# Query parts stored once and repeated by the loads, in an attention and mixture-of-experts layer

## The chip, the cores and the metric
The kernel runs on one core of one Trainium2 chip. The metric is the device time of one execution in microseconds, and the median of several executions is quoted. A core has five engines that run their own streams of instructions and meet at semaphores: TensorE (PE), VectorE (DVE), ScalarE (ACT), GpSimd (POOL) and SyncE (SP). SP does no arithmetic here; it issues nearly all DMAs. 16 DMA engines move the data.

## The reference
One layer on x of 32 batches x 512 tokens x 256. Attention with 16 heads of 16 in 4 key groups (4 query heads share a key head), rotary positions and a causal mask, then a mixture of 16 experts of which each token uses 2:

```python
q = (x @ Wq + bq).reshape(b, t, 16, 16).transpose(0, 2, 1, 3)
k = (x @ Wk + bk).reshape(b, t, 4, 16).transpose(0, 2, 1, 3)   # v likewise
k = jnp.repeat(k, 4, axis=1)
q, k = _rope(q), _rope(k)
scores = jnp.einsum('bhtd,bhsd->bhts', q, k) / scale
scores = jnp.where(causal, scores, -jnp.inf)
attn = jnp.einsum('bhts,bhsd->bhtd', softmax(scores), v)
...
x = x + layernorm(attention(layernorm(x)))
x = x + layernorm(ffn(layernorm(x)))
```

## The kernel before
Each query and key is cut into PARTS = 3 bf16 numbers whose sum is the float32 value. TensorE forms a score as a sum of six products of parts. For that the parts are stacked along the partitions, in six blocks of DH = 16: a tile of 96 partitions (KR) of queries, `qs`, against one of keys, `ks`. BLOCKS says which part of the query and of the key stands in each block:

```python
BLOCKS = [(0, 1), (0, 0), (0, 2), (1, 0), (1, 1), (2, 0)]
Q_BLOCKS = [slice(0, 3), slice(3, 5), slice(5, 6)]
K_BLOCKS = [slice(1, 6, 2), slice(0, 5, 4), slice(2, 3)]
```

So query part 0 stands in blocks 0 to 2, part 1 in 3 and 4, part 2 in 5. The parts are made elsewhere on the partitions: POOL's `split` writes `q_parts` (two halves of 128 partitions, each half eight of the 16 dimensions times 16 heads) and `k_parts`. They reach their blocks through DRAM: SP's `store_parts` writes them to `q_stack_dram` and `k_stack_dram`, with a copy for each block, and `load_stacks` reads them back with the block and the dimension on the partitions, first `ks` (L531) and then one load for each of four groups g of four heads (L535). Three more partitions, 96 to 98, hold the negated row maxima in parts; `load_negmax` (L540) loads them for two groups at a time, from `k_parts_negmax_t`, of which they are 24 partitions.

The work is software-pipelined over batches. The list TURN is one turn, four groups g times 11 slots e; each engine walks the same list for c in TURNS, and a step has an offset that says for which batch it is done. In turn c the scores for exp (L804, `score_exp`) are those of batch c, the scores whose maxima are taken (L788, `score_max`) those of batch c + 1 for groups 0 to 2 (c for group 3), and the projection and splits (L834 and `split`) those of batch c + 2. `load_stacks(c + 1)` stands at slot (0, 5), the first `score_max` of batch c + 1 at (1, 1), `load_negmax` of the second pair of groups at (1, 5) and its first use at (2, 0); the stores of the query halves stand at (2, 4) and (3, 7), that of the keys at (3, 10), and `load_x_res` just before `load_stacks`. Each engine works its stream strictly in this order. Waits: SP waits in `load_stacks` for all parts of the batch (`parts_stored`) and for the last exp of the batch that used the buffer; TensorE waits in `score_max` for the group's load (`q_stack_loaded`), in `score_exp` for `negmax_loaded`. After the last turn of attention come the rest of the expert tiles, with no loads of stacks.

Of the kernel before, what the change touches and what calls it, by code (L numbers as in the profile page):

```python
# [20 lines left out]
BF16 = mybir.dt.bfloat16  # L21
# [7 lines left out]
B, T, D = 32, 512, 256  # L29
NT = T // P  # L30
NC = D // P
H, G, DH = 16, 4, 16
HG = H // G
E, I = 16, 128
TOKENS = B * T
PARTS = 3
# [4 lines that stand above are left out]
KR = len(BLOCKS) * DH  # L41
# [168 lines left out]
D_TAIL = first_of_tail(FOR_DVE, D_NO)  # L210
A_TAIL = first_of_tail(FOR_ACT, A_NO)
SPLITS = 5
PER_STORE = 16 * 3 * PARTS

LAST_TURN = ALL_TILES + 2 + 12
FINALS_FROM, FINALS_OVER = TILES[0] + 8, LAST_TURN - TILES[0] - 9
# [88 lines left out]
def layer(nc, a, out):  # L305
    ctx = ExitStack()
    with ctx:
        def sb(name, shape, dt=F32):
            return ctx.enter_context(nc.sbuf_tensor(name, shape, dt))

        def sem(name):
            return ctx.enter_context(nc.semaphore(name))

        def dram(name, shape, dt=F32):
            return nc.dram_tensor(name, shape, dt, kind="Internal").ap()


        q_stack_dram = dram("q_stack_dram", [2, len(BLOCKS), DH, H, T], BF16)
        k_stack_dram = dram("k_stack_dram", [2, len(BLOCKS), DH, G, T], BF16)
        h2_dram = dram("h2_dram", [B, T, D])  # L320
        sorted_dram = [dram(f"sorted_dram{k}", [LIST, ROW]) for k in range(2)]
        y_dram = dram("y_dram", [2 * TOKENS + ALL_TILES * P, D])


        wq = sb("wq", [P, NC, 2, P])
        wkv = sb("wkv", [P, NC, P])
        bq = sb("bq", [P, 2])
        bk = sb("bk", [P, 1])
        rope = sb("rope", [P, 4, T])
        wo = sb("wo", [P, NC, D])  # L330
        bo = sb("bo", [P, D])
        gate_w = sb("gate_w", [P, NC, 2 * E])
        act_bias = sb("act_bias", [P, 3])
        wgu = sb("wgu", [P, E + 1, NC, 2 * I])
        wd = sb("wd", [P, E + 1, D])
        ident = sb("ident", [P, P])
        ident_bf = sb("ident_bf", [P, P], BF16)
        mask_max = sb("mask_max", [P, P], BF16)
        mask_exp = sb("mask_exp", [P, P], BF16)
        before = sb("before", [P, P], BF16)  # L340
        ones_bf = sb("ones_bf", [P, P], BF16)
        iota_e = sb("iota_e", [P, E])
        token = sb("token", [P, NT])

        h2_std, h2_mean = sb("h2_std", [P, B, NT]), sb("h2_mean", [P, B, NT])
        tile_no, row_no = sb("tile_no", [P, TQ, E]), sb("row_no", [P, 1])
        first_rows = rope[:, :, :].rearrange("p k t -> p (k t)")[:, 0:ROW]
        counts = sb("counts", [P, NT + 1, E])

        pool_cell, dve_cell = sb("pool_cell", [1, 2]), sb("dve_cell", [1, 2])  # L350
        zero_col = sb("zero_col", [P, 1])

        weights_in = sem("weights_in")
        consts = sem("consts")
        experts_in = sem("experts_in")
        h2_stored = sem("h2_stored")
        doubled = sem("doubled")
        scattered = [sem(f"scattered{k}") for k in range(2)]
        lists_begun = sem("lists_begun")

        tile_plan = sb("tile_plan", [P, 2, 3, TQ])
        keep = ctx
        programs(nc, a, out, locals())


def programs(nc, a, out, v):
# [13 lines left out]
    with ctx:  # L380
        def sb(name, shape, dt=F32):
            return ctx.enter_context(nc.sbuf_tensor(name, shape, dt))
# [4 lines left out]
        def sem(name):  # L387
            return v["keep"].enter_context(nc.semaphore(name))
# [6 lines left out]
        q_parts = sb("q_parts", [P, 2, PARTS, T], BF16)  # L395
# [3 lines left out]
        k_parts = k_parts_negmax_t[0:G * DH]  # L399
        negmax_t = k_parts_negmax_t[G * DH:G * DH + PARTS * 2 * HG, 0:2]  # L400
        qs = sb("qs", [P, 2, H, T], BF16)
# [9 lines left out]
        heads = sb("heads", [P, T // 32, 2 * DH])  # L411
# [51 lines left out]
        parts_stored = [sem(f"parts_stored{k}") for k in range(2)]  # L463
        k_stack_loaded = [sem(f"k_stack_loaded{k}") for k in range(2)]
        q_stack_loaded = [[sem(f"q_stack_loaded{k}{g}") for g in range(G)] for k in range(2)]
# [19 lines left out]
    def _(sp):  # L485
# [22 lines left out]
        def store_parts(b, unit):  # L508
            sp.wait_ge(split_steps, SPLITS * (3 * b + unit + 1))
            if unit == 0 and b >= 2:  # L510
                sp.wait_ge(k_stack_loaded[b % 2], 16 * (b // 2))
                for g in range(G):
                    sp.wait_ge(q_stack_loaded[b % 2][g], 16 * (b // 2))
            for part in range(PARTS):
                if unit < 2:
                    half = slice(unit * DH // 2, (unit + 1) * DH // 2)
                    dst = q_stack_dram[b % 2, Q_BLOCKS[part], half].rearrange("k d h t -> (d h) k t")
                    src = q_parts[:, unit, part, :]
                else:
                    dst = k_stack_dram[b % 2, K_BLOCKS[part]].rearrange("k d g t -> (d g) k t")  # L520
                    src = k_parts[:, part, :]
                n = [Q_BLOCKS, K_BLOCKS][unit == 2][part]
                copies = len(range(n.start, n.stop, n.step or 1))
                sp.dma_start(dst, src.unsqueeze(1).to_broadcast([src.shape[0], copies, T])) \
                    .then_inc(parts_stored[b % 2], 16)

        def load_stacks(b):
            sp.wait_ge(parts_stored[b % 2], PER_STORE * (b // 2 + 1))
            if b >= 2:
                sp.wait_ge(a_taken, A_NO["E", (G - 1, NE - 1), b - 2] + 1)  # L530
            sp.dma_start(ks[0:KR, b % 2], k_stack_dram[b % 2].rearrange("k d g t -> (k d) g t")) \  # L531
                .then_inc(k_stack_loaded[b % 2], 16)
            for g in range(G):
                heads = slice(g * HG, (g + 1) * HG)
                sp.dma_start(qs[0:KR, b % 2, heads], q_stack_dram[b % 2, :, :, heads].rearrange("k d h t -> (k d) h t")) \  # L535
                    .then_inc(q_stack_loaded[b % 2][g], 16)

        def load_negmax(b, pair):
            sp.wait_ge(a_taken, A_NO["mt", pair, b] + 1)
# [53 lines left out]
    def _(pool):  # L593
# [36 lines left out]
        def split(b, unit, stage):  # L630
# [11 lines left out]
            if stage == 1 and unit == 0 and b >= 1:  # L642
                pool.wait_ge(parts_stored[(b - 1) % 2], PER_STORE * ((b - 1) // 2 + 1))
            if stage:
# [127 lines left out]
    def _(pe):  # L772
# [3 lines left out]
        def score_max(b, g, u):  # L776
            j, h0, nh, width, stride = MAX_UNITS[u]
            number = D_NO["M", (g, u), b]
            if u == 0:
                if g == 0:  # L780
                    pe.wait_ge(k_stack_loaded[b % 2], 16 * (b // 2 + 1))
                pe.wait_ge(q_stack_loaded[b % 2][g], 16 * (b // 2 + 1))
            if number >= 2:
                pe.wait_ge(d_taken, number - 1)
            for k in range(nh):
                h = g * HG + h0 + k
                at = k * stride
                pe.matmul(ps_d[:, number % 2, at:at + width], qs[0:KR, b % 2, h, j * P:(j + 1) * P],  # L788
                          ks[0:KR, b % 2, g, 0:width], start=True, stop=False)
                ins = pe.matmul(ps_d[:, number % 2, at + j * P:at + (j + 1) * P], ident_bf[:, :], mask_max[:, :],  # L790
                                start=False, stop=True)
            ins.then_inc(d_full, 1)
# [100 lines left out]
        for c in TURNS:  # L893
            for at, step, arg, ahead in TURN:
                b = c + ahead
                if step == "side" and (c, at) in TILE_IN:
                    tile_turn(TILE_IN[c, at])
                if not has(step, b):
                    continue
                if step == "E":  # L900
                    score_exp(b, *arg)
                elif step == "M":
                    score_max(b, *arg)
                elif step == "P":
                    weigh(b, *arg)
                elif step in FOR_DVE:
                    for_dve(step, arg, b)
                elif step in FOR_ACT:
                    for_act(step, arg, b)
# [419 lines left out]
def expert_phases(nc, a, out, v):  # L1329
# [89 lines left out]
    def front_is_free(eng):  # L1419
# [5 lines left out]
        for k in range(2):  # L1425
            eng.wait_ge(v["parts_stored"][k], PER_STORE * B // 2)

# [530 lines left out]
```

## Time and profile before

| what | value |
|---|---|
| median of 3 runs | 2555.26 us (2533.58 to 2560.37) |
| the profiled execution, its own time | 2581.22 us |
| its span, first to last instruction | 2579.4 us |
| mean granted TensorE clock | 0.968 |
| TensorE, DVE, POOL, ACT busy | 91%, 77%, 65%, 55% of the span |
| DMA moved | 387.60 MB, mean 150 GB/s |

The profiled execution has 2 us around its span, and took 26 us more than the median of the runs. Busy shares are averages over two stages, attention (to about 1750 us) and experts; what a change in attention is worth must be read from turns of that stage. In the rows below a name such as `x<-in_x` gives what is written and what is read; L plus a number is a line of the kernel; SPq means an issue by SP.

### The profile page before, as it was taken

The numbers are of one execution on the slowest core, as the hardware profiler recorded it, in microseconds if no ns is written. First come the engines' busy times: TensorE is split into PE (matmuls) and PEld (weight loads), VectorE is DVE, ScalarE is ACT, GpSimd is POOL, SyncE is SP. The second block draws the span as 40 slices with busy tenths as digits, with TensorE's granted clock in tenths as the row PEclk, the third lists the DMA queues.
The fourth block names the chain that finished last, engine by engine and source line by source line (L and its number), as shares of the span: only waits on it lengthen the run. The fifth ranks groups of instructions, "written<-read, shape, count | busy, mean of one in ns | idle before, by whom it ended". The sixth has DMA issues, their size and how long they took to land.

```text
span 2579.4 us, 58722 instructions
## 1 busy us (share of the span) xinstructions
PE 2335.8 (91%) x18042; PEld 1502.2 (58%) x18042; DVE 1985.7 (77%) x5145; ACT 1417.2 (55%) x3248; POOL 1682.2 (65%) x2888
## 2 busy tenths in 40 slices
PE   4969999999999999998999999998779999999987
PEld 2545555555555555555555555554557787777754
DVE  5758888888888888888888888885455555788778
ACT  1546566665666656665566655665334444555544
POOL 2536667767677667766677756653656665677766
PEclk7889999999999999999999999998989999999999
DMA  4355544455444554455434445332344465677757
GB/s 127 89 146 150 158 143 134 129 153 167 129 130 147 156 153 128 121 147 152 122 116 125 141 136 154 109 106 88 113 140 140 147 201 186 194 232 223 230 196 248
DMA packets 289392, 387.60 MB, mean 150 GB/s; under 512 B 25856, under 2 KB 239872, under 8 KB 288960
## 3 DMA queue, kind: packets, MB, share of 16 engines
q1 hardware_dynamic: 263072, 312.51, 41.9%
q0 software_dynamic: 26016, 71.34, 7.5%
q8 instruction: 154, 2.52, 0.4%
q14 instruction: 150, 1.23, 0.2%
HBM read 193.14 MB, written 172.26 MB: 142 GB/s over the span
## 4 chain that ended last, share of the span: by engine, by line
PE 39%; POOL 31%; DMA 11%; issue 9%; DVE 5%; SPq 2%; ACT 1%; another core or an unknown queue 1%; POOLq 0%; ACTq 0%; DVEq 0%
PE bank L1611 9%; DMA qs<-q_stack_dram 7%; PE bank L1625 5%; POOL q_parts L646 4%; PE ps_d L834 4%; POOL rest L648 4%; DMA k_stack_dram<-k_parts_negmax_t 3%; PE ps_d L841 3%; PE ps_d L788 3%; PE bank L1593 2%; POOL sorted_dram L715 2%; POOL guess L686 2%; POOL k_parts_negmax_t L646 2%; POOL q_parts L648 2%; POOL heads L726 2%
## 5 line engine op out<-in xcount | busy, mean ns | idle before, releaser
L931 ACT ACTIVATE probs<-ps_a 128x512 f32<-128x512 f32 (+1 forms) x1408 | 716.2, 560 | 497.4 <-PE ps_a L806 446.0
L1053 DVE TENSOR_REDUCE negmax<-ps_d 128x2 f32<-128x768 f32 (+3 forms) x768 | 779.4, 1033 | 173.3 <-PE ps_d L790 159.2
L788 PE MATMUL ps_d<-ks,qs 96*128 96x128 bf16 (+3 forms) x2048 | 492.6, 307 | 125.0 <-DMA qs<-q_stack_dram 57.7
L804 PE MATMUL ps_a<-qs,ks 99*128 99x512 bf16 (+3 forms) x2048 | 525.2, 304 | 8.6 <-ACT probs L931 2.2
L790 PE MATMUL ps_d<-mask_max,ident_bf 128*128 128x128 bf16 x2048 | 400.6, 224 | 0.0
L806 PE MATMUL ps_a<-mask_exp,ident_bf 128*128 128x128 bf16 x2048 | 391.5, 221 | 0.0
L788 PEld LDWEIGHTS ps_d<-ks,qs 96*128 96x128 bf16 x2048 | 204.7, 100 | 294.1 <-issue 134.3
L1523 POOL DMA_INDIRECT y_dram<-ysb,to_row x286 | 285.6, 999 | 105.3 <-POOL pool_cell L251 52.4
L818 PE MATMUL ps_out<-probs,va 128*32 128x512 f32 (+3 forms) x4096 | 332.9, 443 | 2.5 <-DVE by_token L1096 2.3
L804 PEld LDWEIGHTS ps_a<-qs,ks 99*128 99x128 bf16 x2048 | 199.9, 98 | 207.0 <-issue 65.3
L1611 PE MATMUL bank<-wgu,rows_t 128*128 x1144 | 300.3, 386 | 0.0
L715 POOL DMA_INDIRECT sorted_dram<-h,slot x256 | 256.5, 1002 | 66.0 <-issue 65.1
L1826 DVE TENSOR_TENSOR hid<-bank,gate 128x128 f32<-128x128 f32 x286 | 82.2, 287 | 192.2 <-ACT gate L1731 174.9
L806 PEld LDWEIGHTS ps_a<-mask_exp,ident_bf 128*128 128x128 bf16 x2048 | 202.2, 99 | 28.2 <-issue 20.7
L1625 PE MATMUL bank<-wd,hid_t 128*128 x572 | 181.2, 399 | 40.4 <-issue 21.4
L1611 PEld LDWEIGHTS bank<-wgu,rows_t 128*128 128x128 f32 x1144 | 198.4, 194 | 16.1
L790 PEld LDWEIGHTS ps_d<-mask_max,ident_bf 128*128 128x128 bf16 x2048 | 204.9, 100 | 0.4 <-issue 0.3
L818 PEld LDWEIGHTS ps_out<-probs,va 128*32 128x32 f32 x4096 | 108.1, 110 | 144.9 <-issue 78.5
L251 POOL TENSOR_TENSOR pool_cell<-zero_col 1x1 f32<-1x1 f32 x318 | 62.4, 196 | 196.9 <-DVE slot L1192 105.6
L726 POOL TENSOR_TENSOR heads<-by_token,inverse 128x256 f32<-128x256 f32 x128 | 80.7, 630 | 147.7 <-DVE inverse L1098 141.6
L1731 ACT ACTIVATE gate<-bank 128x128 f32<-128x128 f32 x286 | 79.7, 279 | 139.0 <-PE bank L1611 96.6
L1625 PEld LDWEIGHTS bank<-wd,hid_t 128*128 128x128 f32 x572 | 102.4, 192 | 84.9 <-issue 74.0
(206 smaller groups left out, 4409.3 us busy)
## 6 DMA issues: line engine op xcount, KB each, us to landing
qs<-q_stack_dram SPq DMA_DIRECT2D x128, 384.0 KB
rows<-sorted_dram SPq DMA_DIRECT2D x286, 129.0 KB
y_in<-y_dram SPq DMA_DIRECT2D x32, 1024.0 KB
q_stack_dram<-q_parts SPq DMA_DIRECT2D x64, 384.0 KB, 2.6
x_in<-in_x SPq DMA_DIRECT2D x32, 512.0 KB
q_stack_dram<-q_parts SPq DMA_DIRECT2D x64, 256.0 KB, 2.9
x<-in_x SPq DMA_DIRECT2D x32, 512.0 KB, 4.4
h_dram<-h SPq DMA_DIRECT2D x32, 512.0 KB
```

What stands on the lines that cost most here:

```text
L646: steps.did(pool.tensor_tensor(parts[k], r, zero_col[0:n, :].to_broadcast([n, T]), ALU.add))
L715: pool.indirect_dma_start(out=sorted_dram[b // SPLIT_AT][:, :], in_=h2[:, k, j, :], in_offset=None, out_offset=bass.IndirectOffsetOnAxis(a ...
L788: pe.matmul(ps_d[:, number % 2, at:at + width], qs[0:KR, b % 2, h, j * P:(j + 1) * P], ks[0:KR, b % 2, g, 0:width], start=True, stop=False)
L790: ins = pe.matmul(ps_d[:, number % 2, at + j * P:at + (j + 1) * P], ident_bf[:, :], mask_max[:, :], start=False, stop=True)
L804: pe.matmul(ps_a[:, number % 3, at:at + width], ks[0:KM, b % 2, g, j * P:(j + 1) * P], qs[0:KM, b % 2, g * HG + h0 + k, j * P:T], start=Tr ...
L806: ins = pe.matmul(ps_a[:, number % 3, at:at + P], ident_bf[:, :], mask_exp[:, :], start=False, stop=True)
L818: ins = pe.matmul(ps_out[32 * h:32 * h + 32, j * P:T], va[:, b % 3, j, g * 32:(g + 1) * 32], probs[:, at:at + width], start=(j == 0), stop ...
L931: act.activation(probs[:, at:at + nh * width], ps_a[:, number % 3, 0:nh * width], ACT.Exp) \
L1053: dve.tensor_reduce(negmax[:, g // 2, j, at:at + nh], src, AX_X, ALU.max, negate=True) \
L1523: pool.indirect_dma_start(out=y_dram[:, :], in_=ysb[:, k, :], in_offset=None, out_offset=bass.IndirectOffsetOnAxis(ap=to_row[k][:, 0:1].bi ...
L1611: ins = pe.matmul(ps_gu[t % 2][:, 0:2 * I], rows_t[:, t % 2, c, :], wgu[:, expert[t], c, :], start=(c == 0), stop=(c == NC - 1))
L1625: pe.matmul(ps_y[t % 2][:, 0:D], hid_t[:, t % 2, :], wd[:, expert[t], :], start=True, stop=True) \
```

## The change
A half of the query parts is stored by one transfer that writes the three parts once each, in place of three transfers that write six copies. `q_stack_dram` shrinks from six blocks to three parts. Each group's load becomes three loads, one for each part; the one of part 0 writes 48 partitions and reads its 16 rows three times, that of part 1 writes 32 and reads twice, that of part 2 writes 16. All three count on the semaphore of the group. The keys are stored and loaded as before.

```diff
-PER_STORE = 16 * 3 * PARTS
+PER_STORE = 16 * (2 + PARTS)
...
-        q_stack_dram = dram("q_stack_dram", [2, len(BLOCKS), DH, H, T], BF16)
+        q_stack_dram = dram("q_stack_dram", [2, PARTS, DH, H, T], BF16)
...
+            if unit < 2:
+                half = slice(unit * DH // 2, (unit + 1) * DH // 2)
+                sp.dma_start(q_stack_dram[b % 2, :, half].rearrange("k d h t -> (d h) k t"), q_parts[:, unit]) \
+                    .then_inc(parts_stored[b % 2], 16)
+                return
             for part in range(PARTS):
-                if unit < 2:
-                    half = slice(unit * DH // 2, (unit + 1) * DH // 2)
-                    dst = q_stack_dram[b % 2, Q_BLOCKS[part], half].rearrange("k d h t -> (d h) k t")
-                    src = q_parts[:, unit, part, :]
...
             for g in range(G):
                 heads = slice(g * HG, (g + 1) * HG)
-                sp.dma_start(qs[0:KR, b % 2, heads], q_stack_dram[b % 2, :, :, heads].rearrange("k d h t -> (k d) h t")) \
-                    .then_inc(q_stack_loaded[b % 2][g], 16)
+                for part, n in enumerate(Q_BLOCKS):
+                    sp.dma_start(qs[n.start * DH:n.stop * DH, b % 2, heads],
+                                 q_stack_dram[b % 2, part, :, heads].unsqueeze(0)
+                                 .to_broadcast([n.stop - n.start, DH, HG, T])) \
+                        .then_inc(q_stack_loaded[b % 2][g], 16)
...
-                pe.wait_ge(q_stack_loaded[b % 2][g], 16 * (b // 2 + 1))
+                pe.wait_ge(q_stack_loaded[b % 2][g], 16 * PARTS * (b // 2 + 1))
```

Only SP's stream changes; the other engines have the same instructions in the same order. The first place is SP's stores of one batch, from the load of x to the first store of keys. Before (the sizes are those of the side written, partitions first):

```order
L545 DMA x_in<-in_x 128x4x256
L524 DMA q_stack_dram<-q_parts 128x3x512
L524 DMA q_stack_dram<-q_parts 128x2x512
L524 DMA q_stack_dram<-q_parts 128x512
L540 DMA qs<-k_parts_negmax_t 3x8x512
L524 DMA q_stack_dram<-q_parts 128x3x512
L524 DMA q_stack_dram<-q_parts 128x2x512
L524 DMA q_stack_dram<-q_parts 128x512
L524 DMA k_stack_dram<-k_parts_negmax_t 64x3x512
```

And now:

```order
L547 DMA x_in<-in_x 128x4x256
L516 DMA q_stack_dram<-q_parts 128x3x512
L542 DMA qs<-k_parts_negmax_t 3x8x512
L516 DMA q_stack_dram<-q_parts 128x3x512
L523 DMA k_stack_dram<-k_parts_negmax_t 64x3x512
```

Each half's three stores are one; its 3 is now the number of parts and no longer that of copies of part 0. The load of the maxima keeps its place. The second place is SP's loads of the stacks of one batch, behind the key stores. Before:

```order
L524 DMA k_stack_dram<-k_parts_negmax_t 64x3x512
L524 DMA k_stack_dram<-k_parts_negmax_t 64x2x512
L524 DMA k_stack_dram<-k_parts_negmax_t 64x512
L531 DMA ks<-k_stack_dram 96x2048
L535 DMA qs<-q_stack_dram 96x2048 x4
L545 DMA x_in<-in_x 128x4x256
```

And now, up to the end of the first group:

```order
L523 DMA k_stack_dram<-k_parts_negmax_t 64x3x512
L523 DMA k_stack_dram<-k_parts_negmax_t 64x2x512
L523 DMA k_stack_dram<-k_parts_negmax_t 64x512
L530 DMA ks<-k_stack_dram 96x2048
L535 DMA qs<-q_stack_dram 48x1x2048
L535 DMA qs<-q_stack_dram 32x1x2048
L535 DMA qs<-q_stack_dram 16x2048
```

The last three rows come three times more, for groups 1 to 3, before the load of x (L547): four issues became twelve.

## Rows read from the trace of the kernel before

**Rows 1.** The page's head: span, then busy time, share and instructions.

```profile
span 2579.4 us, 58722 instructions
PE 2335.8 (91%) x18042; PEld 1502.2 (58%) x18042; DVE 1985.7 (77%) x5145; ACT 1417.2 (55%) x3248; POOL 1682.2 (65%) x2888
```

**Rows 2.** Busy time by stretch: one turn; six microseconds inside the query loads.

```profile
core 0: us, PE busy (x) PEld busy (x) DVE busy (x) ACT busy (x) POOL busy (x), PEclk, DMA share, GB/s
1000.00:1052.60 52.60, 49.70 (x463) 29.54 (x460) 45.69 (x107) 33.06 (x69) 37.34 (x63) 1.00 0.47 137
1003.00:1009.00 6.00, 3.85 (x29) 2.86 (x28) 3.57 (x9) 1.61 (x3) 3.75 (x8) 1.00 1.01 266
```

**Rows 3.** Waits of the whole span: total us, times, longest.

```profile
PE ps_d L788 <- DMA qs<-q_stack_dram: 57.7, 29, 4.0
```

**Rows 4.** The chain that ended last, 990 to 1060: start, us, what.

```profile
997.95 2.44 DMA k_stack_dram<-k_parts_negmax_t
1000.40 0.34 SPq L531
1000.79 6.77 DMA qs<-q_stack_dram
...
1013.98 3.60 PE ps_d L834 x8
...
1053.39 5.90 DMA qs<-q_stack_dram
```

**Rows 5.** TensorE in order of time: start, us, instruction, idle before and releaser.

```profile
1007.65 0.22 PE L788 MATMUL ps_d<-ks,qs 96*128 96x128 bf16 x1 [2.15 <-DMA qs<-q_stack_dram]
...
1021.71 0.39 PE L804 MATMUL ps_a<-qs,ks 99*128 99x512 bf16 x1
```

**Rows 6.** SP's issues in order of time, same turn.

```profile
1000.40 0.34 SPq L531 DMA_DIRECT2D ks<-k_stack_dram  x1
1000.79 2.68 SPq L535 DMA_DIRECT2D qs<-q_stack_dram  x4
1003.52 1.22 SPq L545 DMA_DIRECT2D x_in<-in_x  x1
1015.07 0.79 SPq L540 DMA_DIRECT2D qs<-k_parts_negmax_t  x1
...
1041.07 1.62 SPq L524 DMA_DIRECT2D q_stack_dram<-q_parts  x3
```

**Rows 7.** DVE, then POOL, in order of time, same turn.

```profile
1026.67 0.28 DVE L1034 BATCH_NORM_AGGREGATE moments<-stats 128x2 f32<-128x6 f32 x3
...
1028.05 0.20 POOL L684 TENSOR_TENSOR var<-moments,eps 128x4 f32<-128x4 f32 x1
```

**Rows 8.** DMA packets of the span; queues with packets, MB, share of 16 engines.

```profile
DMA packets 289392, 387.60 MB, mean 150 GB/s; under 512 B 25856, under 2 KB 239872, under 8 KB 288960
q1 hardware_dynamic: 263072, 312.51, 41.9%
q0 software_dynamic: 26016, 71.34, 7.5%
```

**Rows 9.** DMA issues: engine, count, KB each, median us from issue to landing.

```profile
qs<-q_stack_dram SPq DMA_DIRECT2D x128, 384.0 KB
...
q_stack_dram<-q_parts SPq DMA_DIRECT2D x64, 384.0 KB, 2.6
...
q_stack_dram<-q_parts SPq DMA_DIRECT2D x64, 256.0 KB, 2.9
...
q_stack_dram<-q_parts SPq DMA_DIRECT2D x64, 128.0 KB, 2.8
...
qs<-k_parts_negmax_t SPq DMA_DIRECT2D x64, 24.0 KB
```

**Rows 10.** TensorE's restart after the start-up; then windows with granted clock.

```profile
43.11 0.27 PE L788 MATMUL ps_d<-ks,qs 96*128 96x128 bf16 x1 [17.97 <-issue]
...
44.00:48.00 4.00, 3.54 (x19) 2.14 (x17) 2.99 (x4) 0.00 (x0) 0.00 (x0) 0.50 1.02 259
48.00:52.00 4.00, 4.00 (x7) 1.64 (x7) 1.70 (x2) 0.00 (x0) 0.00 (x0) 0.68 0.05 16
```

More of the change, by code:

```diff
@@ L512, in store_parts @@
                 for g in range(G):
-                    sp.wait_ge(q_stack_loaded[b % 2][g], 16 * (b // 2))
-            for part in range(PARTS):
-                if unit < 2:
-                    half = slice(unit * DH // 2, (unit + 1) * DH // 2)
-                    dst = q_stack_dram[b % 2, Q_BLOCKS[part], half].rearrange("k d h t -> (d h) k t")
-                    src = q_parts[:, unit, part, :]
[L519 to L522, printed above, removed]
+                    sp.wait_ge(q_stack_loaded[b % 2][g], 16 * PARTS * (b // 2))
+            if unit < 2:
[3 more added lines that the diff above has]
+                return
+            for part in range(PARTS):
+                n = K_BLOCKS[part]
+                dst = k_stack_dram[b % 2, n].rearrange("k d g t -> (d g) k t")
                 copies = len(range(n.start, n.stop, n.step or 1))
-                sp.dma_start(dst, src.unsqueeze(1).to_broadcast([src.shape[0], copies, T])) \
+                sp.dma_start(dst, k_parts[:, part, :].unsqueeze(1).to_broadcast([G * DH, copies, T])) \
                     .then_inc(parts_stored[b % 2], 16)
```

## The prediction

> **What bounds the kernel now.** I read the page's head first: TensorE is busy for 2335.8 of 2579.4 us [rows 1]. In the attention stage one batch is one turn of 52.6 us, and in a turn it is busy for 49.7 [rows 2]. That looks like a TensorE bound, so I went on to the waits. TensorE waits 29 times for the load of the query stack, 57.7 us in all, 2.0 us each [rows 3]. The chain of work in time shows how that wait is made, and that it closes a loop from turn to turn: the query projection (L834) feeds DVE and then some 30 us of POOL splits, the last store of key parts lands 2.44 us after its issue, SP issues the load of the key stack and then that of the first query group, and 6.77 us later (5.90 in the next turn) TensorE goes on [rows 4]. So two things of nearly equal length hold a turn: TensorE's own work, and this loop through POOL and two DMA round trips. Whatever lengthens the first group's load lengthens the loop by as much, from the first microsecond on. What shortens it helps by 2 us a turn at most, since then TensorE's work is the bound.
>
> **How a transfer is laid on the DMA engines.** This decides the case. The only transfer of the kernel before whose two sides differ in their outer size is that of the row maxima (L540): 3 partitions of 8 rows on one side, 24 partitions on the other. Each engine that takes part adds one small packet at the end of a transfer, and these can be counted. SP issues 1086 transfers and POOL 542 indirect ones (the sum of the counts of the DMA view; the loops give the same), 64 of them L540 [rows 9], and 640 data packets (rows of bk, bq, act_bias and gate_w) are under 512 B. The page has 25856 packets under 512 B [rows 8]. With 16 engines for all: 640 + 16 x 1628 = 26688, which is 832 = 64 x 13 too many. With 3 engines for each L540 it comes out to the packet. So a transfer is cut by the outer sizes as its patterns list them, and is not spread over the 24 rows that it has. The new loads list 48 partitions on the side of qs and an outer step of 3 (the repeat, then 16 rows) on the side of DRAM, and 32 with 2 for the second part. If both sides count, these run on 3 and on 2 engines. If the destination alone did (the row fits that too), they would run on 16. I take the first, because a share must be whole on both sides and L540's source with 24 was held to 3.
>
> The Trainium skill, "DMA: Bandwidth & Descriptors", section "Why a DMA increments its semaphore by 16 and not by 1", speaks against this change: the number of engines is the largest up to 16 that divides the outermost sizes of both patterns, and they are the lowest-numbered ones. By it the new loads have 3 and 2 engines, and by it L540 has 3, with which the packet count agrees; no row here shows the numbers of the engines.
>
> **What the change removes.** Per batch four of six q stores and 768 of 1536 KB written ([rows 9]: 384 + 256 + 128 KB a half become 384). I cost the saving at nothing: the q1 stores are issued at 1041.07 in 1.62 us [rows 6], while the key parts that the loads wait for are stored when POOL is done with them, so that the next query load is issued only at 1053.39 [rows 4]. What hides the stores is POOL's chain. Bound of a gain: emptier engines might let the key store land sooner than its 2.44 us; stores of 384, 256 and 128 KB land in 2.6, 2.9 and 2.8 [rows 9], so size does little, and I allow 0.2 us a turn, 6 us.
>
> **What it adds, in issues.** Eight more issues a batch on SP, at 2.68 us for four [rows 6] 0.67 us each or less. Two of them stand in the first group's load, 1.3 us, beside transfers that take longer: nothing. Behind them in SP's queue stand the load of x and L540, 11.5 us later [rows 6].
>
> **What it adds, in time of the engines.** Bytes and rows of 4 KB are as before: 96 rows a group. Before, each engine had 6 of them. Now the two lowest engines have 16 + 16 + 1 = 33. Price of a row: between 1003 and 1009 only such loads run, at 266 GB/s with a share of 1.01 [rows 2], so 16.5 GB/s an engine and 0.25 us for 4 KB, all 16 pulling at once. In the light traffic of the indirect queue, 71.34 MB took 7.5% of 16 x 2579.4 = 3095 us [rows 8]: 23.0 GB/s, 0.178 us. With three engines at work the new load is nearer to the second; I take 0.178 and keep 0.25 as the far end. By the same skill page's section "Specifications" (about 27 GiB/s an engine) a row would be 0.141 us and the whole sum about 140 us in place of the 323 below; no row here shows that rate.
>
> First term, **the load of group 0**. From the issue of the key load (call it S, 1000.40) to TensorE's restart (1007.65) are 7.25 us [rows 5, 6]. Of these the engine worked on 6 rows of ks and 6 of q, 12 x 0.25 = 3.0; 4.25 us are start, rest of an earlier load, and completion. After: 4.25 + (6 + 33) x 0.178 = 4.25 + 6.9 = 11.2. So +3.9 us, on the loop, with nothing to hide it (far end: 39 x 0.25 gives +6.75).
>
> Second term, **the row maxima behind the query loads**. L540 for the second pair is issued at S + 14.7 [rows 6] and uses the same engines. In the turn shown TensorE does not wait for it before [rows 5]. Now the lowest engine has first 6 + 4 x 33 = 138 rows, 24.6 us; the load of x, 32 rows of 1 KB, 1.4; six of POOL's eight scatters a turn, which stand at slots (0, 9) and (0, 10) (26016 / 542 = 48 packets each [rows 8], of which 32 data: 2 an engine), 12 x 0.178 = 2.1; its own 8 rows, 0.4. With 4.25 that is S + 32.8. TensorE needs it for the first exp scores of group 2, 14.06 us after its restart (1021.71 - 1007.65, [rows 5]), so at S + 25.3. It waits 7.5 us. Of that, does the loop feel it? DVE's moments, which stand behind the next maxima, are ready at 1026.95 and POOL takes them at 1028.05 [rows 7]: 1.1 us of slack, then POOL's chain is late by 6.4. What is queued behind the waiting matmul is all of TensorE's stream, with DVE's maxima and POOL's splits. (Far end at 0.25: ready at S + 44.3, needed at S + 28.1, 16.2 of wait, 15.1 on the loop. Near end: nothing reaches the loop.)
>
> Groups 1 to 3 land 33 x 0.178 = 5.9 us apart and are needed a quarter of a turn, 13 us, apart: no wait.
>
> Third term, **the clock**. After an idle stretch of 17.97 us TensorE restarts at 43.11 at granted 0.50, and 48 to 52 has 0.68 [rows 10], so full speed from about 50.6: 7.4 us at 1.2 GHz, 3.7 lost. After the 2.15 us wait it was at 1.00 [rows 2, 5]. Two waits of 6 and 7.5 us a turn lie between these rows. I take 0 and keep 2 x 3.7 a turn, 229 us, as the other bound.
>
> **Sum.** 3.9 + 6.4 = 10.3 us a turn; 31 turns with both terms and one with the first: 319 + 4 = 323 us. The expert stage is not touched. Against the profiled execution, 2581.2 + 323 = 2904; it stood 26 us over the median of 2555.3, and against the median I forecast **2878 us**.
>
> **Rivals.**
> - Only the first term counts: the maxima come late, but the turn has grown and POOL had more air than I give it. 32 x 3.9 = 125, so 2680. Against it: no slack over 1.1 us in [rows 7].
> - Everything dearer: the clock falls at each wait (2878 + 229 = 3107), or a row stays at 0.25 us (31 x 21.9 + 7 = 686, so 3241). For it: the low clock after the start. Against it: only three engines pull.
> - Other side, **the loads are spread over all 16 engines** because the destination's 48, 32 and 16 decide. It decides as soon as the engine count of the first part is 16. Then the transfers are as before, the stores are halved, and the time is between -6 us (landing of the key parts) and +43 (32 x 1.34 us, if the two more issues delay the first group in full): 2549 to 2598, likeliest near 2565. For it: the packet count fits this reading too. Against it: L540's 24 rows did not help it, and its rule would have to ignore one side.
> - That the change moves other bytes than it says is excluded by the shapes: 128x3x512 stored, 48, 32 and 16 rows of 2048 loaded.
>
> **How the numbers follow.** Forecast (three engines, both terms, clock or price partly in it, 2760 to 3110) 0.65; first term only or little more (2620 to 2760) 0.15; dearer than 3110, 0.09; spread over 16, 0.11. The range that leaves out the last two is 2660 to 3110. A difference under 1% (25 us) can't be told from none here, with runs from 2533.6 to 2560.4. Slower by over 1%: 0.65 + 0.15 + 0.09 and 0.03 of the last case, 0.92; within 1%: 0.06; faster: 0.02.
>
> **What would show it.** In the profile after: packets under 512 B. 128 stores fewer take 2048 away, and the loads have (3 + 2 + 16) x 128 = 2688 in place of 2048, so 24448; spread over 16 it would be 27904. TensorE's wait for qs<-q_stack_dram about 6 us, 32 times, and a new wait for qs<-k_parts_negmax_t, 31 times, about 7. The DMA share falls from about 1.0 to 0.2 for some 20 us after the loads' issue. A turn of 63 us. If turns are 56 to 57, the second term is wrong; if the share stays at 1.0 in the loads, the first step is; if granted clock in attention falls well below 0.97, the third term is in play.

## The result, and the profile after

The changed kernel takes 2827.39 us (2824.37 to 2836.7), against 2557.41 us for the kernel before with one more run counted (2533.58 to 2560.37). The ratio, taken over all runs, is 1.109 of the kernel before (95% interval 1.102 to 1.115); the quotient of the medians is 1.106. The forecast was 2878, slower. Its profiled execution has a span of 2822.6 us, against 2579.4 [rows 1]. The kernels of the experiments ran on chips on which the kernel before took 2580 to 2590 us, so each is compared by its ratio to the kernel before on the same chip.

The page after, its head and its DMA rows (they answer to [rows 1] and [rows 8]):

```profile
span 2822.6 us, 58850 instructions
PE 2405.7 (85%) x18042; PEld 1568.4 (56%) x18042; DVE 1993.2 (71%) x5145; ACT 1424.1 (50%) x3248; POOL 1680.7 (60%) x2888
...
DMA packets 263410, 362.44 MB, mean 128 GB/s; under 512 B 24449, under 2 KB 213889, under 8 KB 262977
...
q1 hardware_dynamic: 237088, 287.34, 33.9%
q0 software_dynamic: 26016, 71.34, 6.8%
```

The packets under 512 B are read first, since they tell how the new loads are laid out: 24449, where 3 and 2 engines ask for 24448 and 16 engines for 27904. 25 MB fewer were moved, and nothing came of it.

The waits of the whole span (us in total, times, longest), to be held against [rows 3]:

```profile
POOL var L686 <- DVE moments L1036: 373.5, 92, 30.7
...
PE ps_d L790 <- DMA qs<-q_stack_dram: 161.6, 29, 7.1
...
PE ps_a L806 <- DMA qs<-k_parts_negmax_t: 108.6, 31, 8.0
```

The query load is waited for 5.6 us each time in place of 2.0, 103.9 us more. The wait for the row maxima is new but for 0.2 us: 31 times, 3.5 us. Together these waits are 212.5 us; the span grew by 243.2. TensorE's busy time also grew, by 69.9 us, with the same number of instructions, and its other waits shrank. DVE and POOL have no more work than before; the time in which POOL waits for DVE's moments grew from 100.5 us to 373.5, which is how TensorE's lateness reaches the loop.

The chain of work in order of time, through one turn (start, us, what; [rows 4] is its match):

```profile
1035.05 2.43 DMA k_stack_dram<-k_parts_negmax_t
1037.50 0.34 SPq L530
1037.88 0.77 SPq L535
1038.70 0.68 SPq L535
1039.42 8.76 DMA qs<-q_stack_dram
1048.27 0.26 PE ps_d L790
...
1057.31 10.27 DMA qs<-k_parts_negmax_t
1067.63 0.39 PE ps_a L806
```

From the issue of the key load, 1037.50, to TensorE's restart are 10.77 us where they were 7.25. The chain now runs a second time through a DMA: the load of the row maxima, 24 KB, takes 10.27 us from its issue. The explanation, tested below, is that it stands behind the query loads in the queues of its three engines. TensorE's stream (idle before, and what ended it) and POOL's, in the same turn:

```profile
1048.27 0.26 PE L790 MATMUL ps_d<-ks,qs 96*128 96x128 bf16 x1 [5.67 <-DMA qs<-q_stack_dram]
...
1067.63 0.39 PE L806 MATMUL ps_a<-qs,ks 99*128 99x512 bf16 x1 [2.48 <-DMA qs<-k_parts_negmax_t]
...
1073.79 0.20 POOL L686 TENSOR_TENSOR var<-moments,eps 128x4 f32<-128x4 f32 x1 [2.34 <-DVE moments L1036]
```

Before, POOL took the moments 20.40 us after TensorE's restart [rows 5, 7]; now 25.52. With 3.5 us from the first wait, 5.1 from there to the moments and 0.6 behind them, the turn has 61.9 us in place of 52.6. The view by stretches shows the turn and the pieces after its two waits (the columns of [rows 2]):

```profile
1037.50:1099.40 61.90, 53.66 (x464) 32.83 (x461) 45.93 (x107) 33.31 (x70) 37.38 (x64) 0.92 0.37 111
1040.00:1048.00 8.00, 2.59 (x14) 1.65 (x11) 2.95 (x9) 1.19 (x2) 5.18 (x9) 0.97 0.51 155
1048.00:1052.00 4.00, 3.73 (x21) 3.04 (x22) 1.56 (x2) 0.60 (x1) 1.92 (x2) 0.50 0.51 169
1052.00:1057.00 5.00, 5.00 (x40) 3.37 (x39) 2.77 (x6) 1.76 (x4) 0.00 (x0) 0.77 0.51 157
1057.00:1062.00 5.00, 5.00 (x26) 2.67 (x24) 4.78 (x12) 1.58 (x4) 2.47 (x8) 1.00 0.28 95
...
1067.00:1072.00 5.00, 4.37 (x29) 3.12 (x30) 2.03 (x4) 2.03 (x4) 4.21 (x4) 0.66 0.09 26
```

Two things are to be seen. The DMA share while the loads run, 0.51, is half of what it was [rows 2], although as many bytes are asked for. And the granted clock is 0.50 (1.2 GHz) for the 4 us after the wait of 5.67 us, and low again (0.66 in the mean of 5 us) after the second wait, of 2.48 us: the same matmuls take longer just where the loop hangs on them.

### The profile page after: what moved, and what is told of

It reads as the page before. It is cut to its first block, busy times and chain, and to the rows that moved or that the text cites. A ratio compares the mean times of both kernels' runs of the same rounds, so it can differ in the third digit from the quotient of the medians.

```text
span 2822.6 us, 58850 instructions
## 1 busy us (share of the span) xinstructions
PE 2405.7 (85%) x18042; PEld 1568.4 (56%) x18042; DVE 1993.2 (71%) x5145; ACT 1424.1 (50%) x3248; POOL 1680.7 (60%) x2888
## 2 busy tenths in 40 slices
DMA packets 263410, 362.44 MB, mean 128 GB/s; under 512 B 24449, under 2 KB 213889, under 8 KB 262977
## 4 chain that ended last, share of the span: by engine, by line
PE 48%; DMA 24%; POOL 12%; issue 6%; DVE 5%; SPq 4%; ACT 1%; POOLq 0%; ACTq 0%; DVEq 0%
DMA qs<-k_parts_negmax_t 12%; DMA qs<-q_stack_dram 9%; PE bank L1613 8%; PE ps_d L790 6%; PE ps_a L806 6%; PE bank L1627 4%; PE ps_out L820 4%; PE ps_d L843 3%; PE ps_d L792 3%; DMA k_stack_dram<-k_parts_negmax_t 3%; PE ps_d L836 3%; POOL k_parts_negmax_t L648 2%; PE bank L1595 2%; PE ps_a L808 2%; SPq L523 2%
## 5 line engine op out<-in xcount | busy, mean ns | idle before, releaser
L790 PE MATMUL ps_d<-ks,qs 96*128 96x128 bf16 (+3 forms) x2048 | 541.1, 330 | 216.9 <-DMA qs<-q_stack_dram 161.6
L806 PE MATMUL ps_a<-qs,ks 99*128 99x512 bf16 (+3 forms) x2048 | 553.9, 319 | 116.7 <-DMA qs<-k_parts_negmax_t 108.6
L792 PE MATMUL ps_d<-mask_max,ident_bf 128*128 128x128 bf16 x2048 | 444.0, 241 | 0.0
L790 PEld LDWEIGHTS ps_d<-ks,qs 96*128 96x128 bf16 x2048 | 224.3, 110 | 389.9 <-issue 267.8
L808 PE MATMUL ps_a<-mask_exp,ident_bf 128*128 128x128 bf16 x2048 | 402.9, 226 | 0.0
L806 PEld LDWEIGHTS ps_a<-qs,ks 99*128 99x128 bf16 x2048 | 206.2, 101 | 322.5 <-DMA qs<-k_parts_negmax_t 130.8
L686 POOL TENSOR_TENSOR var<-moments,eps 128x4 f32<-128x4 f32 x96 | 19.3, 201 | 375.8 <-DVE moments L1036 373.5
L792 PEld LDWEIGHTS ps_d<-mask_max,ident_bf 128*128 128x128 bf16 x2048 | 224.5, 110 | 0.4 <-issue 0.3
L808 PEld LDWEIGHTS ps_a<-mask_exp,ident_bf 128*128 128x128 bf16 x2048 | 208.2, 102 | 28.2 <-issue 21.2
L1627 PE MATMUL bank<-wd,hid_t 128*128 x572 | 179.4, 396 | 28.7 <-issue 19.1
L843 PE MATMUL ps_d<-wo,headst 128*128 128x256 f32 x512 | 158.3, 463 | 0.8 <-DVE place L1179 0.8
```

What stands on the lines that cost most here:

```text
L806: pe.matmul(ps_a[:, number % 3, at:at + width], ks[0:KM, b % 2, g, j * P:(j + 1) * P], qs[0:KM, b % 2, g * HG + h0 + k, j * P:T], start=Tr ...
L808: ins = pe.matmul(ps_a[:, number % 3, at:at + P], ident_bf[:, :], mask_exp[:, :], start=False, stop=True)
L843: ins = pe.matmul(ps[:, k * D:(k + 1) * D], headst[:, c, j * P:(j + 1) * P], wo[:, c, :], start=(c == 0), stop=(c == NC - 1))
L1627: pe.matmul(ps_y[t % 2][:, 0:D], hid_t[:, t % 2, :], wd[:, expert[t], :], start=True, stop=True) \
```

## The experiments

To compare turns, I took from SP's issues in order of time all issues of the key load between 300 and 1700 us and the first matmul of the new batch behind each; the last such turn of each kernel is left out, and the means are in this table. "Restart" is the time from the key load's issue to that matmul, "maxima" that to TensorE's restart after the wait for the row maxima.

| kernel | ratio to before (95%) | turn us | restart | maxima |
|---|---|---|---|---|
| before | 1 | 53.6 | 6.9 | no wait |
| changed | 1.109 (1.102 to 1.115) | 62.5 | 10.6 | 30.4 |
| no_repeat | 1.109 (1.104 to 1.114) | 62.6 | 10.9 | 30.5 |
| spread_repeat | 1.0065 (1.0043 to 1.0086) | 54.2 | 7.1 | no wait |
| three_plain_loads | 1.0051 (1.0033 to 1.0069) | 54.3 | 7.3 | no wait |
| six_loads | 1.0079 (1.0056 to 1.0102) | 54.4 | 7.3 | no wait |
| six_engines | 1.0307 (1.0265 to 1.0349) | 56.4 | 8.6 | no wait |
| maxima_between | 1.0662 (1.0621 to 1.0703) | 58.7 | 11.1 | no wait |
| first_spread | 1.0749 (1.0707 to 1.0791) | 60.6 | 6.9 | 27.9 |
| keep_busy | 1.1003 (1.0957 to 1.1049) | 62.1 | 11.0 | mostly no wait |
| between_busy | 1.0539 (1.0513 to 1.0564) | 58.0 | 11.1 | no wait |
| stacks_first | 0.9882 (0.9842 to 0.9922) | 52.6 | 5.6 | no wait |
| stacks_first_spread | 0.9986 (0.9972 to 1.0000) | 53.1 | 6.6 | no wait |

My theory was that the outer sizes 3 and 2 in the source confine the loads to a few engines, and that the loss is two waits behind the queue of these engines. The rivals were that a row read three times is what costs, that it is the number of issues, that only the first wait matters, and that the low clock does.

**No repeat, still few engines.** The stores of the kernel before, with a padding row behind each block so that the blocks can't be joined into one run of rows:

```diff
-        q_stack_dram = dram("q_stack_dram", [2, len(BLOCKS), DH, H, T], BF16)
+        q_stack_dram = dram("q_stack_dram", [2, len(BLOCKS), DH + 1, H, T], BF16)
...
+                for n in Q_BLOCKS:
+                    sp.dma_start(qs[n.start * DH:n.stop * DH, b % 2, heads], q_stack_dram[b % 2, n, 0:DH, heads]) \
+                        .then_inc(q_stack_loaded[b % 2][g], 16)
```

> The stores of the kernel before (six copies), three loads a group as in the changed kernel, but each load reads its own copies: the blocks in DRAM lie one padding row apart, so that the source still lists an outer size of 3 (or 2) and no row is read twice. If the few engines are the cause: as the changed kernel, 2827 us within 30, with waits for the query load near 5.6 us each and for the row maxima near 3.5. If reading one row three times were what costs: back at 2557 us.

Ratio 1.109, as the changed kernel. Its waits:

```profile
PE ps_d L789 <- DMA qs<-q_stack_dram: 168.5, 29, 6.9
...
PE ps_a L805 <- DMA qs<-k_parts_negmax_t: 97.2, 31, 4.8
```

Each row is read once and six copies are stored, and the loss is whole. The repeat is not the cause, nor are the stores any part of it. The packets under 512 B are 26496, which is the 25856 of the kernel before [rows 8] and 640 more: 128 loads on 16 engines have become 128 times 3, 2 and 16 engines.

**The repeat, on 16 engines.** Here the repeat stays and the confinement goes. The partitions of a part are ordered by dimension first and copy second, and the keys alike:

```diff
-                                 q_stack_dram[b % 2, part, :, heads].unsqueeze(0)
-                                 .to_broadcast([n.stop - n.start, DH, HG, T])) \
+                                 q_stack_dram[b % 2, part, :, heads].unsqueeze(1)
+                                 .to_broadcast([DH, n.stop - n.start, HG, T])) \
...
-            sp.dma_start(ks[0:KR, b % 2], k_stack_dram[b % 2].rearrange("k d g t -> (k d) g t")) \
-                .then_inc(k_stack_loaded[b % 2], 16)
+            for n in Q_BLOCKS:
+                sp.dma_start(ks[n.start * DH:n.stop * DH, b % 2], k_stack_dram[b % 2, n].rearrange("k d g t -> d k g t")) \
+                    .then_inc(k_stack_loaded[b % 2], 16)
```

> Stored once and repeated by the loads as in the changed kernel, but the source lists the 16 dimensions first and the repeat inside, so that both sides divide by 16; the key stack is loaded in the same order of partitions, by three loads in place of one. If the few engines are the cause: 2557 us within 40 (10 SP issues more a batch than in the kernel before, half the bytes stored), waits for the query load about 2 us each, none for the row maxima. If the repeat or the number of issues is the cause: 2800 or more.

Ratio 1.0065. Its packets, and TensorE's wait for the query load (that for the maxima is 0.3 us, once):

```profile
DMA packets 267889, 362.46 MB, mean 139 GB/s; under 512 B 28928, under 2 KB 218368, under 8 KB 267456
...
PE ps_d L791 <- DMA qs<-q_stack_dram: 59.5, 28, 2.8
```

59.5 us of wait, as in the kernel before (57.7), and 28928 packets under 512 B, which is what 16 engines for each load make: 128 stores and 160 loads fewer and 480 loads more than before, at 16 each, 25856 + 192 x 16. The same idea in another order of two sizes costs about a seventeenth of the loss. With the first experiment this settles the cause, and it also shows that the idea was worth nothing: half the query bytes stored, ten issues more a batch, and not faster.

**Three plain loads a group**, each with its own copies and flat rows, in the kernel before:

```diff
...
+                for n in Q_BLOCKS:
+                    sp.dma_start(qs[n.start * DH:n.stop * DH, b % 2, heads],
+                                 q_stack_dram[b % 2, n, :, heads].rearrange("k d h t -> (k d) h t")) \
...
```

> The kernel before with each group's load cut into three by partitions (48, 32, 16), each with its own copies and flat rows, so that each runs on 16 engines: eight more issues a batch and nothing else. If issues cost nothing: 2557 us within 10. If two more issues delay the first group by their own time: up to 43 us more, 2600. If the issues were the cause of the whole loss: 2827.

Ratio 1.0051, 13 us for eight more issues a batch, 0.4 us a turn. The restart is 0.3 us later.

**Six loads a group**, 20 more issues a batch, in the changed kernel:

```diff
-                for part, n in enumerate(Q_BLOCKS):
...
+                for n, (part, _) in enumerate(BLOCKS):
+                    sp.dma_start(qs[n * DH:(n + 1) * DH, b % 2, heads], q_stack_dram[b % 2, part, :, heads]) \
+                        .then_inc(q_stack_loaded[b % 2][g], 16)
```

> The changed kernel with each group loaded by six loads of 16 partitions without a repeat, all on 16 engines: 20 more issues a batch than in the kernel before, half the bytes stored. If issues ahead of group 0 cost their own time (five more at 0.5 us): 2.5 us a turn less what the transfer hides, 1.01 to 1.03 of the kernel before. If issues hide beside the transfers: 1.00 to 1.007, as with eight or ten more.

1.0079: between my two expectations' ranges, and within its interval of the 1.0065 with ten more. Issues hide beside the transfers nearly in full.

**Six engines.** The padding row alone, with one load a group whose source lists 6 outside:

```diff
-                sp.dma_start(qs[0:KR, b % 2, heads], q_stack_dram[b % 2, :, :, heads].rearrange("k d h t -> (k d) h t")) \
+                sp.dma_start(qs[0:KR, b % 2, heads], q_stack_dram[b % 2, :, 0:DH, heads]) \
```

> The kernel before, with one padding row behind each of the six blocks in DRAM and nothing else: one load a group still, but its source lists an outer size of 6, so it runs on 6 engines with 16 rows each (6 before, up to 33 in the changed kernel). If the rows on the busiest engine set the price: group 0 is late by (22 x 0.17) - 3.0 = 0.7 us a turn, the row maxima come at about 20 us after the key load's issue and are not waited for, and the time is 1.01 of the kernel before, between 1.005 and 1.02. If any confinement cost as much as in the changed kernel: 1.10.

1.031, and the packets confirm the six engines, 128 x 10 fewer under 512 B than the 25856 before:

```profile
DMA packets 288112, 387.60 MB, mean 146 GB/s; under 512 B 24576, under 2 KB 238592, under 8 KB 287680
```

So there is a smaller loss with six engines than with three, but it is three times what I expected. The restart is late by 1.7 us, not by 0.7: with the 4.25 us of start and completion kept, as in the first term of the prediction, a row comes to 0.20 us here, (8.6 - 4.25) / 22, and not to the 0.17 that I had put in. The turn grew by 2.9. From its restart to the exp scores of group 2 TensorE takes 16.2 us in the mean, where the kernel before takes 14.9; the granted clock is 0.951 in the mean, in a kernel whose waits are 3.5 us each (100.9 us, 29 times). How much of the difference the clock makes, this run doesn't tell. There is no wait for the maxima, as expected.

**Only the first wait.** Groups 2 and 3 are loaded behind the row maxima:

```diff
...
-                    load_stacks(c + 1)
+                    load_stacks(c + 1, (0, 1))
+                if at == (1, 5) and exists(c + 1):
+                    load_stacks(c + 1, (2, 3))
```

> The changed kernel with the loads of groups 2 and 3 issued behind the load of the row maxima in place of before it. If the two waits are two terms: the wait for the row maxima of the second pair goes (108.6 us in the profile after), that for group 0 stays at 5.6 us each, and the time is 2827 less 80 to 130, about 2720. If the second wait had cost nothing on the loop: 2827. If groups 2 and 3 now come late: a new wait for the query load at groups 2 or 3.

1.066. The wait for the maxima is gone: issued at the same time as in the changed kernel (19.3 us behind the key load, 19.1 there), they land 2.7 us after their issue and no longer 11.3 us after it (means of the same turns). The loads of groups 2 and 3 in front of them were what held them up. The wait for the query load is 175.3 us:

```profile
PE ps_d L793 <- DMA qs<-q_stack_dram: 175.3, 29, 7.2
```

**Only the second wait.** Group 0 is loaded by six loads on 16 engines, the others as in the changed kernel:

```diff
+                if g == 0:
+                    for n, (part, _) in enumerate(BLOCKS):
+                        sp.dma_start(qs[n * DH:(n + 1) * DH, b % 2, heads], q_stack_dram[b % 2, part, :, heads]) \
+                            .then_inc(q_stack_loaded[b % 2][g], 16)
+                    continue
```

> The changed kernel, with group 0 alone loaded by six loads of 16 partitions (no repeat, 16 engines); groups 1 to 3 stay on 3 and 2 engines. If the two waits are two terms of one queue: the wait for the query load is back near 2 us, the row maxima land 27 rows x 0.16 = 4.3 us sooner after the key load's issue but are needed 3.5 us sooner too, so that wait stays at 3 to 4 us; together 1.04 to 1.05 of the kernel before. If only the wait for group 0 mattered: 1.01.

1.075, where I had 1.04 to 1.05:

```profile
PE ps_a L811 <- DMA qs<-k_parts_negmax_t: 169.2, 31, 8.0
...
PE ps_d L795 <- DMA qs<-q_stack_dram: 55.3, 28, 3.2
```

The maxima land only 2.5 us sooner (27.9 against 30.4), not 4.3, and are wanted 5.0 us sooner: TensorE comes to them 6.0 us before they land in the mean of these turns, so at 21.9, where the changed kernel comes at 26.9 (30.4 - 3.5). It restarts 3.7 us earlier, and gets on faster from there. Each wait alone costs 6.6% and 7.5%, both together 10.9%: the first one pushes back the time at which the second transfer is needed, so they do not add up. The turn says the same. In the kernel before TensorE comes to these scores at 21.9 us in the mean, with nothing to wait for; in the changed kernel it can do them at 30.4, when the maxima land, and 8.5 us later is nearly all of the 8.9 by which the turn grew. Once the maxima are that late, a sooner restart gains only what it takes off the landing: 2.5 us here, and the turn is shorter by 1.9.

**The clock.** Matmuls without use fill the waits, into a slot that is overwritten next: in the changed kernel 80 ahead of the first wait (the edit is shown) and 45 ahead of the second, and in the kernel with the maxima between the 80 alone:

```diff
+                    if number >= 2:
+                        pe.wait_ge(d_taken, number - 1)
+                    for _ in range(80):
+                        pe.matmul(ps_d[:, number % 2, 0:P], ident_bf[:, :], mask_max[:, :], start=True, stop=True)
                     pe.wait_ge(k_stack_loaded[b % 2], 16 * (b // 2 + 1))
...
```

> The changed kernel, with 80 matmuls of 128 columns that TensorE does ahead of its wait for group 0 and 45 ahead of its wait for the row maxima of the second pair, into the PSUM slot that is overwritten next: they fill the waits, at some 4.5 and 2.5 us, and change no result. If the low clock after the waits costs time of its own: granted clock near 0.97 again and up to 2 x 2 us a turn less, down to 2700. If the time that the low clock costs behind group 0 would be spent in the wait for the maxima anyway: clock up, time 2827 less 0 to 60. If the fillers end after the loads land: slower than 2827.

> The kernel with the row maxima between the loads (groups 2 and 3 behind them), with 80 matmuls of 128 columns that TensorE does ahead of its wait for group 0 and whose result is overwritten. Here no second wait can take back what is won behind the first. If the low clock behind the wait costs time on the loop: granted clock near 0.97 and 0.98 to 0.99 of that kernel, so 1.045 to 1.055 of the kernel before. If TensorE's lower speed there hides beside POOL and DVE: the same 1.066.

In the changed kernel the granted clock rises from 0.923 to 0.963, and the ratio is 1.100 (1.096 to 1.105) against 1.109 (1.102 to 1.115): the intervals overlap, so little or nothing is won. With the maxima between, the clock rises from 0.937 to 0.971 and the ratio falls from 1.066 to 1.054, outside both intervals. By stretches, the kernel with the maxima between and then the same with the filler:

```profile
300.00:1500.00 1200.00, 1056.27 (x9417) 634.79 (x9418) 941.83 (x2195) 675.52 (x1390) 769.30 (x1297) 0.94 0.37 113
```

```profile
300.00:1500.00 1200.00, 1137.90 (x11151) 713.11 (x11150) 953.81 (x2240) 686.02 (x1412) 773.89 (x1304) 0.99 0.38 115
```

DVE, whose work is the same in each turn, did 953.81 us of it in place of 941.83 in the same 1200 us. So the low clock after the first wait is worth 25 to 32 us, 0.8 us a turn by the turns and 1 by the ratios, where nothing takes it back. In the changed kernel what is won in front of the maxima is lost: they land 30.5 us after the key load's issue with the fillers and 30.4 without, whether TensorE is quick or slow on its way to them.

But the run with both fillers does not show what the clock costs in the changed kernel, because the second filler is too long. In 15 of 21 turns it ends after the maxima have landed. In one such turn, whose key load is issued at 1093.59 and whose maxima land at 1124.4, the chain runs through the filler and not through their load:

```profile
1122.67 2.62 PE ps_a L808 x45
1125.29 0.22 PE ps_a L815
```

In the mean TensorE restarts at 31.5 us, 1.1 later than in the changed kernel, and the rest of the turn takes 30.6 us where it took 32.1. So about 1.5 us a turn are won behind the second wait, and the filler takes most of them back. A shorter filler was not tried; by these rows it would bring a turn of about 61.1 us (30.5 + 30.6), an estimate.

**A kernel faster than both.** The chain says that what stands in front of group 0 on the DMA queues is on the loop. In the kernel before, the residual x (512 KB) is issued ahead of the stacks and needed only at slot (1, 9), 17 slots after its own. One number moves it behind them:

```diff
-    "load_x_res": (0, 3),
+    "load_x_res": (0, 5),
```

> The kernel before, with the load of the residual x (512 KB) issued behind the loads of the stacks in place of 1.8 us before them. If the DMA queue in front of group 0 is on the loop: the load lands up to 2 us sooner, the wait of 2.0 us a turn shrinks to 0.5 or less, and the time is 0.98 to 0.99 of the kernel before. If TensorE's own work is all that bounds a turn by now: 1.00.

0.988 (0.984 to 0.992). The restart comes after 5.6 us in place of 6.9, and the wait of 57.7 us [rows 3] is

```profile
PE ps_d L788 <- DMA qs<-q_stack_dram: 16.8, 20, 1.9
```

The same with the parts stored once and repeated on 16 engines:

> Stored once, the loads repeat the parts with the 16 dimensions outermost (16 engines), and the load of the residual x behind the loads of the stacks. If the two changes add up: 0.988 x 1.0065 = 0.994 of the kernel before. If storing half the bytes pays once the queue in front of the loads is short: 0.985 or less.

0.9986 (0.9972 to 1.0000): no gain of the stored bytes here either, and the twelve query loads and three key loads give back a percent of what the move brought, a restart after 6.6 us in place of 5.6.

## Why the prediction was right, point by point

**How the transfer is laid out** was right and carried the rest: 24449 packets under 512 B with 24448 forecast. By the rule for the number of engines that the Trainium skill's page "DMA: Bandwidth & Descriptors" gives ("Why a DMA increments its semaphore by 16 and not by 1"), the same change with the sizes in the other order has 16 engines. The trace agrees, with 28928 packets under 512 B, and the ratio is 1.0065.

**What is removed at nothing**: right. On 16 engines two kernels that store once (1.0065, 1.0079) are no faster than the one that stores all copies (1.0051).

**Issues at nothing**: nearly. Eight more cost 0.5%, 13 us, which the sum left out. They had been priced at 0.67 us each or less; the twelve took 10.59 us in the turn shown, 0.88 each.

**First term**, +3.9 us: the restart moved by 3.7 (6.9 to 10.6). With the 4.25 us of start and completion kept, (10.6 - 4.25) / 39 = 0.16 us for a row of 4 KB, where I took 0.178.

**Second term**, 7.5 us of wait and 6.4 on the loop: the mechanism was right, with a wait of 3.5 us. Of the 4.0 us too many, 2.4 are the landing (30.4 us after the key load's issue, not 32.8; take off the same 4.25, 1.4, 2.1 and 0.4 and 138 rows have 0.16 us each again), and 1.6 that TensorE comes to it at 26.9 and not at 25.3. It needs 16.3 us from its restart in the mean and not 14.1. Of these 2.2 us, 0.8 were there before the change: the 14.06 were read from one turn, and the mean of the kernel before is 14.9. The other 1.4 go with the low clock; with the maxima between, the fillers take 0.8 of such a delay back (16.0 us become 15.2). On the loop the term has 5.1 us in the turn shown, since that slower stretch lies in it as well; the two errors partly cancel.

**Third term**, the clock, was taken as 0 between 0 and 7.4 us a turn. It does fall, and 0 was too low. By the fillers its worth is 0.8 to 1 us a turn when the second wait is gone, and about 1.5 behind the second wait in the changed kernel, the last from one pair of runs with a filler that ended late. In front of the second wait it costs nothing on the loop as far as the landings show (30.5 and 30.4); I had not seen that a slow TensorE and a late transfer cover each other.

**The sum**: 323 us forecast, 270 measured, 8.4 us for each of 32 turns, and 8.9 by the turns themselves, where 10.3 was forecast. The two terms do not stand side by side as I added them. What the loop feels is one difference: the landing of the maxima less the time at which TensorE came to them before, less POOL's slack, 32.8 - 21.3 - 1.1 = 10.4 in the prediction's numbers. Measured, the landing is 2.4 us sooner, by the price of a row; TensorE came to them 0.6 us later before than in the turn that I read; and in place of 1.1 us gained from slack 0.4 was lost (32.1 us from the maxima to the next key load, where it was 31.7), which the 1.5 us of low clock behind the second wait would explain. That gives 8.9. The term that was off in size is the second, and that the sum came within 20% of the measured loss is in part luck: the row was priced too high and the clock at nothing.

**What the profile was to show**: waits of about 6 us for the query load (5.6, 29 times) and of 7 for the maxima (3.5, 31 times); a turn of 63 us (61.9 in the one shown, 62.5 in the mean). The granted clock fell from 0.968 to 0.923, the sign that I had named for the third term. Wrong was the DMA share of 0.2 during the loads: it was 0.51. I had counted only the three engines and not that the loads of x, the third load of each group and POOL's scatters go on using the others. In the trace from 1041 to 1057 us, packets of 4 KB (the stacks) have half of the engines' busy time, those of the scatters over a quarter and those of 1 KB (x) a fifth.

## What to carry to other kernels

Before folding copies into a transfer, look at the outermost size that each side of its pattern lists: 3 against 48 makes a load of 16 engines one of three, and putting the 16 outside and the repeat inside undoes that at no cost in bytes. A transfer on few engines also holds up every later small one that shares them, so look for what is issued next and needed soon. Cut bytes only where the trace shows a wait for them; in this kernel the order of two loads was worth 1.2%, and half of the query stores nothing that could be measured.

## What the runs showed of the hardware beyond what was expected

- A row of 4 KB from DRAM costs an engine 0.16 us here when three carry the load (from two separate landings; the packets of 4 KB between 300 and 1700 us have a median of 0.161 us), against 0.25 us when all 16 pull ([rows 2]; median 0.249 in the same stretch of the kernel before). Three engines are therefore slower than 16 by less than their number says: group 0 by 3.7 us and not by 6.75.
- Transfers on few engines stand in each other's way: the load of the maxima (24 KB, 3 engines) lands 11.3 us after its issue behind four groups on 3 and 2 engines, and 2.7 us after it behind two of them, or in the kernel before.
- The granted clock was at 0.50 after a wait of 5.67 us, at 0.66 in the mean of 5 us after one of 2.48, and at 1.00 after one of 2.15 [rows 2, 5]; waits of 3.5 us in the mean (six engines) went with a mean clock of 0.951 against 0.968.
- Two waits in one turn that cost 6.6% and 7.5% alone cost 10.9% together.
